# Attention maxima of a two-layer transformer kernel: turned as float32 at chunk 0, split into halves after the turn, and three pieces at other places in TensorE's step

## The reference, cut to what matters

```python
scores = (einsum(q_cos, k_cos) + einsum(q_sin, k_sin)) / sqrt(8) * exp(log_scale)   # layer 1: q @ k.T / sqrt(8)
scores = where(tril, scores, -inf)
attn = softmax(scores, axis=-1)          # needs each query's maximum
out = (attn @ v).reshape(B, S, 128) @ Wo.T
```

## Time and profile before

| what | value |
|---|---|
| median of 3 runs | 1272.88 us (1272.55 to 1272.88) |
| the profiled execution | 1268.47 us, span 1266.9 us, mean granted TensorE clock 0.897 |
| TensorE busy | 981.7 us (77% of the span) |
| VectorE busy | 819.4 us (65%) |
| ScalarE busy | 690.9 us (55%) |
| GpSimd busy | 582.5 us (46%) |

### The profile page before, as it was taken

How to read it: one execution, slowest core, us unless ns; L and a number is a source line. 1 busy time by engine, 2 the same in 40 slices (tenths; PEclk the granted TensorE clock), 3 DMA queues, 4 the chain that set the end, 5 groups by cost and what they waited for, 6 DMA issues and landing times. The chain is left out here.

```text
span 1266.9 us, 27743 instructions
## 1 busy us (share of the span) xinstructions
PE 981.7 (77%) x8908; PEld 647.1 (51%) x8908; DVE 819.4 (65%) x1770; ACT 690.9 (55%) x1325; POOL 582.5 (46%) x793
## 2 busy tenths in 40 slices
PE   3789652989867988888872655199999599999987
PEld 1456431777753544444431433188888345555553
DVE  1566341667748999999943776133333699999992
ACT  1366343878714777677763454022222277777775
POOL 3467537010112565565551466411110367777775
PEclk9899776999985999999996666599999599999999
DMA  4321042577752222222201434456665112211111
GB/s 134 108 51 51 26 118 74 160 210 225 208 172 77 80 69 69 72 76 62 73 24 36 115 115 119 142 164 194 185 192 163 39 46 54 55 52 51 51 45 30
DMA packets 151735, 126.30 MB, mean 100 GB/s; under 512 B 23760, under 2 KB 134272, under 8 KB 151648
## 3 DMA queue, kind: packets, MB, share of 16 engines
q1 hardware_dynamic: 141904, 107.05, 29.5%
q0 software_dynamic: 8016, 17.71, 4.8%
q10 hardware_dynamic: 1728, 0.46, 0.2%
HBM read 77.83 MB, written 44.70 MB: 97 GB/s over the span
## 5 line engine op out<-in xcount | busy, mean ns | idle before, releaser
L2089 ACT ACTIVATE attend_probs<-attend_attend_ps 128x512 f32<-128x512 f32 x640 | 351.1, 600 | 161.7 <-PE attend_attend_ps L2163 154.4
L2163 PE MATMUL attend_attend_ps<-attend_q,attend_ks 50*128 50x512 f16 (+3 forms) x1024 | 236.5, 307 | 20.1 <-ACT attend_probs L2089 18.0
L2052 POOL TENSOR_SCALAR_AFFINE_SELECT attend_probs<-attend_probs 128x512 f32<-128x512 f32 x256 | 158.7, 637 | 159.5 <-ACT attend_probs L2089 158.6
L2131 PE MATMUL attend_attend_ps<-attend_ks,attend_q 48*128 48x512 f16 (+3 forms) x1024 | 191.3, 317 | 25.5 <-DMA attend_ks<-k_stack 16.2
L2176 PE MATMUL attend_attend_ps<-attend_probs,attend_vals 128*32 128x512 f32 (+3 forms) x2048 | 178.9, 446 | 0.0
L2258 DVE TENSOR_REDUCE attend_neg_max<-attend_attend_ps 128x2 f32<-128x1024 f32 x128 | 155.0, 1211 | 9.9 <-PE attend_attend_ps L2143 9.8
L2143 PE MATMUL attend_attend_ps<-identb,stairs 64*128 64x128 bf16 (+1 forms) x1280 | 144.3, 213 | 0.0
L2163 PEld LDWEIGHTS attend_attend_ps<-attend_q,attend_ks 50*128 50x128 f16 x1024 | 70.9, 94 | 116.1 <-ACT attend_probs L2089 93.2
L2260 DVE TENSOR_REDUCE attend_neg_max<-attend_attend_ps 128x2 f32<-128x768 f32 x128 | 121.8, 951 | 9.2 <-PE attend_attend_ps L2143 8.4
L1800 DVE TENSOR_TENSOR experts_hidden<-experts_experts_ps,experts_gate 128x512 f32<-128x512 f32 x39 | 27.0, 691 | 136.3 <-ACT experts_gate L1779 136.3
L2143 PEld LDWEIGHTS attend_attend_ps<-identb,stairs 64*128 64x128 bf16 x1280 | 105.9, 100 | 17.5 <-issue 4.7
(11 more groups left out here) (319 smaller groups left out, 1950.7 us busy)
## 6 DMA issues: line engine op xcount, KB each, us to landing
experts_w_in<-in_L_ffn_w_dram SPq DMA_DIRECT2D x78, 176.0 KB, 2.4
q_stack<-middle_parts SPq DMA_DIRECT2D x24, 256.0 KB, 3.3
k_stack<-middle_parts SPq DMA_DIRECT2D x24, 256.0 KB, 3.6
attend_q<-q_stack SPq DMA_DIRECT2D x64, 96.0 KB, 2.2
attend_ks<-k_stack SPq DMA_DIRECT2D x64, 96.0 KB, 2.2
middle_w_in<-in_L_ffn_W_dram SPq DMA_DIRECT2D x23, 256.0 KB, 2.7
middle_w_out<-in_L_ffn_W_dram SPq DMA_DIRECT2D x23, 256.0 KB, 3.1
experts_rows<-sorted POOLq DMA_DIRECT2D x39, 128.0 KB, 2.5
```

The source lines that it names most:

```text
L2052: pool.affine_select(out=block_, in_=block_, compare_op=ALU.is_ge, fill=0.0, base=0, pattern=[[0, GH], [1, P]], channel_multiplier=-1).the ...
L2089: act.activation(probs[:, u.par, 2 * c + side, :], ps[:, PROB + side, :], ACT.Exp, scale=SCALE ** -2)\
L2131: pe.matmul(ps[:, bank + side, col:col + (qt + 1) * P], q[rows(side, KR), g, pair, qt * P:(qt + 1) * P], ks[rows(side, KR), g, pair, 0:(qt ...
L2163: mm = pe.matmul(ps[:, PROB + side, col:col + S - kt * P], ks[rows(side, KM), g, pair, kt * P:(kt + 1) * P], q[rows(side, KM), g, pair, kt ...
```

## The change

- `split_maxima`, `max_parts` and the float16 identity `identh` go. `neg_max` is padded with 16 columns of zeros to 32, and `turn_maxima` turns it as float32 with two matmuls into two blocks of 32 partitions of `TURN`, so that the maxima stand there twice.
- ScalarE makes the high parts of all 64 partitions from there (`high_maxima`, 64x128), and VectorE the low ones in place on the second 32 (`low_maxima`, one operation of 32x128 from PSUM and `maxT`). `copy_maxima` goes.
- SyncE writes them with four DMAs for a unit, of one row of `q` each, in place of two with two rows each.
- On TensorE `mix(t-3, ...)` stands at chunks 0, 1 and 2 (2 and 3 at chunk 2), `turn_maxima(t-1)` at chunk 0, `turn_mix(t-4)` at chunk 1 behind a wait for `maxT_ready(t-1)`, `turn_context` at chunk 3.
- On ScalarE the copy to `mixT` stands behind the exponentials of chunk 3, and `high_maxima` behind those of chunk 0. On VectorE `divide(t-4)` stands behind reduce 2 and `low_maxima(t-1)` behind reduce 1.

```diff
-        max_parts = sb("max_parts", [P, 2, 2, 2, HP * QT], F16)
-        maxT = sb("maxT", [2 * GH * QT, 2, P], F16)
+        neg_max = sb("neg_max", [P, 2, 2 * GH * QT])
+        LOW = 2 * GH * QT
+        maxT = sb("maxT", [2 * LOW, 2, P], F16)
...
-                    for side in range(2):
-                        sp.dma_start(q[64 * side + KR:64 * side + KM, u.group, :, :], maxT[16 * side:16 * side + 16, u.par, :])\
-                          .then_inc(max_in[u.par].sem, 16)
+                    for part in range(2):
+                        for side in range(2):
+                            row, first = 64 * side + KR + part, LOW * part + HP * QT * side
+                            sp.dma_start(q[row:row + 1, u.group, :, :], maxT[first:first + HP * QT, u.par, :])\
+                              .then_inc(max_in[u.par].sem, 16)
...
+            def keep_mix(u):
+                act.wait_ge(mixed.sem, mixed.done(u))
+                if u.past(1):
+                    act.wait_ge(mix_turned.sem, mix_turned.done(u - 1))
+                act.copy(mixT[:, :], ps[:, MIX, :]).then_inc(mixT_ready.sem, 1)
+
+            def high_maxima(u):
+                act.wait_ge(max_turned.sem, max_turned.done(u))
+                if u.past(2):
+                    act.wait_ge(max_in[u.par].sem, u.pair * 64)
+                act.activation(maxT[:, u.par, :], ps[0:2 * LOW, TURN, 0:P], ACT.Identity, scale=SHIFT).then_inc(high_done.sem, 1)
...
+                    if c == 0 and active(t, 1, UNITS):
+                        high_maxima(t - 1)
+                    if c == 3 and active(t, 3, UNITS):
+                        keep_mix(t - 3)
...
-                pe.wait_ge(parts_done.sem, parts_done.done(u))
-                pe.matmul(ps[0:2 * GH * QT, TURN, 0:P], max_parts[:, u.par, :, :, :].rearrange("p s a b -> p (s a b)"),
-                          k.identh[:, :], start=True, stop=True)\
-                  .then_inc(max_turned.sem, 1)
+                pe.wait_ge(maxed.sem, maxed.done(u))
+                for part in range(2):
+                    mm = pe.matmul(ps[LOW * part:LOW * (part + 1), TURN, 0:P], neg_max[:, u.par, :], k.ident[:, :], start=True, stop=True)
+                mm.then_inc(max_turned.sem, 1)
...
-                    if c == 0 and active(t, 4, UNITS):
-                        before_mix(t)
-                        turn_mix(t - 4)
-                    if 1 <= c <= 3 and active(t, 3, UNITS):
-                        mix(t - 3, c - 1)
-                        if c == 3:
+                    if active(t, 3, UNITS) and c < 3:
+                        mix(t - 3, c)
+                        if c == 2:
                             mix(t - 3, 3)
-                    if c == 1 and active(t, 1, UNITS):
-                        before_maxima(t)
+                    if c == 0 and active(t, 1, UNITS):
+                        after_mix(t)
                         turn_maxima(t - 1)
-                    if c == 2 and row_ends:
+                    if c == 1 and active(t, 4, UNITS):
                         if active(t, 1, UNITS):
                             pe.wait_ge(maxT_ready.sem, maxT_ready.done(t - 1))
+                        else:
+                            after_mix(t)
+                        turn_mix(t - 4)
+                    if c == 3 and row_ends:
                         turn_context(t - 4)
...
-            def split_maxima(u):
-                flat = neg_max[:, u.par, :, :, :].rearrange("p s h j -> p s (h j)")
-                parts = max_parts[:, u.par, :, :, :]
-                if u.past(2):
-                    dve.wait_ge(max_turned.sem, max_turned.done(u - 2))
-                dve.wait_ge(maxed.sem, maxed.done(u))
-                dve.tensor_scalar(parts[:, :, 0, :], flat, SHIFT, None, ALU.mult).then_inc(high_done.sem, 1)
+            def low_maxima(u):
                 dve.wait_ge(high_done.sem, high_done.done(u))
-                dve.scalar_tensor_tensor(out=parts[:, :, 1, :], in0=flat, scalar=SHIFT, in1=parts[:, :, 0, :],
-                                         op0=ALU.mult, op1=ALU.subtract).then_inc(parts_done.sem, 1)
+                low = maxT[LOW:2 * LOW, u.par, :]
+                dve.scalar_tensor_tensor(out=low, in0=ps[LOW:2 * LOW, TURN, 0:P], scalar=SHIFT, in1=low,
+                                         op0=ALU.mult, op1=ALU.subtract).then_inc(maxT_ready.sem, 1)
...
-                    if c == 0 and active(t, 4, UNITS):
+                    if c == 1 and active(t, 1, UNITS):
+                        low_maxima(t - 1)
+                    if c == 2 and active(t, 4, UNITS):
                         divide(t - 4)
-                    if c == 1 and active(t, 1, UNITS):
-                        copy_maxima(t - 1)
```

55 lines of the change are left out of this document (17 added, 38 removed).

## The result

The changed kernel takes 1386.93 us (median of six runs, 1381.91 to 1392.76), the kernel before 1272.57 us in the runs beside it: **ratio 1.0901, 95% interval 1.0869 to 1.0932**, or 114 us more. The forecast was 1327 us, with a range up to 1350. The sign was right and so was the main wait; the size, 54 us, was less than half of what came.

What follows compares the result with a forecast made beforehand. It took TensorE's pieces alternating with ScalarE's exponentials as the bound. Full rows add 52 us and filling 2, so the profiled 1268.47 us becomes 1322.5; with 4.4 us to the runs' median, the forecast was 1327 us, range 1298 to 1350.

Steps and rivals of the forecast that it cites:

- three waits: TensorE, each step: 0.85 us at turn_mix, 0.4 ahead of chunk 4, about 0.8 more ahead of chunk 0; 2.05 in all.
- rival 1: VectorE is the only bound, so its relief makes the kernel faster: 48 us less, 1225 us; chance 0.05.
- T0 to T1: TensorE, chunk 0's start to chunk 1's: chunk 0 0.70, mix 0 0.88, float32 turn of the maxima 0.22; 1.80 us.
- T1 to T2: TensorE, chunk 1's start to chunk 2's: 2.86 us, with 0.85 waiting for VectorE's low_maxima and 0.56 for turn_mix.
- T2 to T3 and T3 to T0: TensorE: chunk 2 with mix 2 and 3, 1.40 us; chunk 3 to next chunk 0, behind exponentials and mixT copy, 2.57.
- Step 8.63: One full TensorE step: 1.80 + 2.86 + 1.40 + 2.57 = 8.63 us, against 7.23 before.
- row-end step: Step with turn_context, its copy and project: 1.17 us more with 0.2 back, entered as 1.0 a row.
- layer norm: Layer 0: VectorE's layer norm makes GpSimd's masks late, holding up low_maxima; 1.2 us a row.
- Filling: Steps 2 and 3 of each layer: the four DMAs are not hidden, 1 us a layer, 2 in all.
- The lock: VectorE/GpSimd shared port: low_maxima stays free, no hold-up costed; if held, up to 1.0 us a row, 14 in all.
- the sum: Whole kernel: seven rows a layer, 7 x (4.25 + 3.2) = 52 us more, 54 with filling.
- Rival 4: TensorE's clock falls to 1.2 GHz from idling, some 240 us over 56 steps: 1560 us; chance 0.02.

Runs made afterwards that it cites:

- after: The changed kernel itself, against the kernel before: 1386.93 us, ratio 1.0901.
- e11: Changed kernel with TensorE's steps of both attentions written out without a loop; ratio to the kernel before 1.0713.
- e13: Changed kernel with low_maxima ahead of reduce 1 and TensorE's attention steps without a loop, both turns kept; ratio to the kernel before 1.0254.
- e3: Changed kernel with low_maxima ahead of reduce 1, not behind it; ratio to the kernel before 1.0386.
- e4: Changed kernel with the copy to mixT between the two exponentials of chunk 4; ratio to the kernel before 1.1035.
- e10: Changed kernel with five unread matmuls of 384 columns ahead of TensorE's wait at turn_mix; ratio to the kernel before 1.0915.
- e17: Kernel before with TensorE's attention steps written without a loop; ratio to the kernel before 0.9987.
- e2: Changed kernel with one float32 turn of the maxima in place of two, on a chip with late starts; ratio to the kernel before 1.0924.
- e12: Changed kernel with low_maxima ahead of reduce 1 and one float32 turn in place of two, loop kept; ratio to the kernel before 1.0204.
- e15: Changed kernel with one float32 turn in place of two, repeated on another chip; ratio to the kernel before 1.0740.
- e1: Kernel before with the float16 turn of the maxima issued four times in place of once; ratio to the kernel before 1.0149.
- e6: Maxima made as in the changed kernel, pieces in the order of the kernel before; ratio to the kernel before 1.0395.
- after_again: Changed kernel repeated unchanged; ratio to the kernel before 1.0913.
- e8: Maxima made as in the kernel before, pieces in the order of the changed kernel; ratio to the kernel before 1.0874.
- e9: Changed kernel's maxima in the kernel before's order, one float32 turn, high parts' transfers issued once ScalarE is done; ratio to the kernel before 1.0102.
- e16: Layer 0 in old order with new maxima, one float32 turn, early high-part transfers, TensorE unrolled; layer 1 as in the kernel before; ratio to it 0.9994.

## Why the prediction came out as it did

Against the kernel before, in shares of its time (1% is 12.7 us), the 0.0901 can be taken apart in two orders. Loop first: TensorE's fetch with the slow clock behind it is 0.0188 (after against e11), then the wait at `turn_mix` 0.0459 (e11 against e13). Wait first: 0.0515 (after against e3), then the fetch 0.0132 (e3 against e13). Either way e13's 0.0254 is left, for the waits for exponentials, the row-end, the filling and the turn. That each order sums to 0.0901 is so by construction and proves nothing; that the two differ by 0.0056 says how far the shares can be told apart.

- **What bounds it, and where the waits stand: right.** Each of the three waits is where it was put. VectorE's relief (rival 1) gave nothing here: it idles 0.84 and 1.39 us in a step.
- **T0 to T1, 1.80: measured 2.01.** `turn_maxima` takes 0.32 (1130.31 to 1130.63), not 0.22, and chunk 0 with `mix` 0 takes 1.69, not 1.58.
- **T1 to T2, 2.86: measured 3.04.** Chunk 1's reduction starts 0.79 after its scores, as laid out, but L2276 starts 1.32 behind it, not 1.19: L2270's 0.44 to the next start was read as 0.33. The wait is 0.94, not 0.85. In e3 it is gone.
- **T2 to T3 and T3 to T0, 1.40 and 2.57: measured 1.40 and 2.55.** The reasoning that the copy to `mixT` was a loss by its place falls all the same: e4 shows the second exponential right behind it.
- **Step 8.63: measured 9.00,** 0.37 more, 21 us over 56 steps. With the row-end step and layer 0's layer norm a row without fetches (e11) takes 37.26 and 38.70 us where 35.5 and 36.8 were forecast (the terms of the latter give 36.7): 26 us over seven rows of each.
- **Filling, 1 us a layer: 5.3.** From the first scores to chunk 0 of step 4 it took 33.15 us in layer 1 (1048.40 to 1081.55) and 33.43 in layer 0, where it took 27.69 (994.39 to 1022.08) and 28.22 before. The first landing of four transfers holds chunk 0 of layer 1 for 2.77 us, the next two for 1.24 and 1.41. In full steps the transfers stayed hidden but in a few, as the sum from the earlier trace rows had it.
- **The lock: right.** L2276 takes 0.28 us in all 64 cases, beside GpSimd's additions too. By the Trainium skill (SBUF — State Buffer, Who interferes with whom) it should be free of the lock, and the trace agrees.
- **With these sizes the forecast would have been 89 us more than before** (54, 26 and 9): e11, which has the changed kernel's order and no loop, measured 0.0713, 91 us.
- **Two steps failed.** The first is the sizes of the terms: T0 to T1 and T1 to T2 (21 us), the row-end step and the layer norm (5) and the filling (9) were too small by 35 us together, and e11's 1363.21 us, with no fetch in it, is already outside the range. The second is "the sum": that nothing stands beside the step's own pieces. The prediction counted what each added instruction takes, and put at nothing, without a reason, what a changed TensorE program does to its loop of eight steps. That is worth 24 us (after against e11): four waits of 3.0 to 3.7 us (13.5) and the slow clock after them. Rival 4 had the clock, but as all or nothing (1560 us) and from idle time at the waits; e10 and e11 show that those waits do not drop it in layer 1 (1.00 in e11). In layer 0 the clock stays at 0.97 even unrolled; what drops it there is open.
- **The Trainium skill (Runtime: NRT & Kernel Launch, Instruction fetch mechanics)** says that a taken branch whose target is outside the part held forces a fetch before the engine goes on. The 3.64 us at the jump back, and e11 and e17, agree with it. That rule leaves open why the same program waited at four jumps in one execution and at three in another.

What decides whether the loop is fetched anew is not settled. By the turn products in a turn of the loop, 8 before and 16 in e2, e12 and e15 went without a fetch, and 32 in the changed kernel, e1 and e3 to e6 met one, at every jump back but one of after_again. But e8 with 8 and e9 with 16 fetch as well, each in one layer only. And e16's layer 1 is the kernel before's own code, loop and all, with other code of layer 0 ahead of it: it fetches at one jump, 4.43 us, where the kernel before does at none in two traces. So length alone does not decide; what stands ahead of the loop seems to count, and after_again shows that the program does not fix all of it.

## What to carry to other kernels

Where an engine must hand over a small result, ask what stands ahead of it in that engine's own order: 0.28 us of work behind a reduction that itself waits for the receiver's scores cost 65 us here, and nothing when issued one piece earlier. When a change touches a long loop or the code ahead of it, look at the instruction queue's packets and at waits for "issue" at the jump back, and unroll both kernels as a test. And when a wait is taken away on paper, work out the second in line, with its distance: moving the copy won 0.39 us at one exponential and gave more back at the next (9.09 us a step in place of 9.00).

## What the hardware showed that was not expected

- With 48 small instructions more in TensorE's loop (e1) the jumps back cost 2.7 to 3.6 us and 37 more instruction packets came. The kernel before's own loop met 4.43 us at one jump when only the layer ahead of it was changed (e16).
- After a 3.64 us gap TensorE ran 5 us at 1.2 GHz; 0.9 us gaps in every step of attend1 left it at 2.4 GHz (e11).
- On one chip 19 of 71 of VectorE's waits for TensorE in layer 1 ended over 0.5 us after the shown end of the releaser, by up to 1.4 us (e2); on another 3 of 58, by up to 0.76 (e15). The rows of layer 1 were 6 us longer there, with 55 us at 1.2 GHz in place of 3: far more than the second turn, which the run was to price.
